# Attention inside an expert pipeline: turned probabilities and value sums by pairs of tiles

## The reference, cut to what matters

```python
x = x + attn(cond(x, ...), ...)          # scores, causal mask, softmax, value sums, W_o
h = einsum('bsd,bdh->bsh', x, W[cat_ids]) + b[cat_ids]
for wg, wu, wdn, cw in experts:          # all 64, weighted by a routing that is zero for most
    y += cw[:, None] * ((silu(h @ wg) * (h @ wu)) @ wdn)
x = x + y + shared(h)
```

## Time and profile before

| | us |
|---|---|
| median of 3 runs | 749.6 (747.75 to 752.17) |
| the profiled execution | 748.22 |
| its span | 746.4 |
| PE busy | 721.3 (97%) |
| DVE, ACT, POOL busy | 549.0, 453.5, 425.1 |
| mean granted clock of TensorE | 0.995 of full |

### The profile page before, as it was taken

The page is one execution under the profiler, slowest core; times in us unless marked ns, Lnnn a source line. Parts: engine busy times, 40 slices in busy tenths (PEclk is TensorE's granted clock), DMA queues, the critical chain, the costliest instruction groups (busy, mean ns, idle before and its releaser), DMA issues.

```text
span 746.4 us, 15904 instructions
## 1 busy us (share of the span) xinstructions
PE 721.3 (97%) x5680; PEld 560.0 (75%) x5680; DVE 549.0 (74%) x1150; ACT 453.5 (61%) x873; POOL 425.1 (57%) x349
## 2 busy tenths in 40 slices
PE   8877999999999999999999999999999999999997
PEld 6765776677777777777787777777777777887885
DVE  5796668886698756976778766987668766886664
ACT  3755865477556675567555774566754675555553
POOL 2528667566456545655555654666446564566665
PEclk9999999999999999999999999999999999999999
DMA  7495443435534453444564344443634345345441
GB/s 264 141 356 135 123 121 99 127 94 156 120 107 118 123 144 109 129 103 127 125 117 134 98 150 113 120 113 120 141 113 135 103 125 128 102 125 141 128 134 46
DMA packets 69055, 97.21 MB, mean 130 GB/s; under 512 B 8016, under 2 KB 26896, under 8 KB 68976
## 3 DMA queue, kind: packets, MB, share of 16 engines
q1 hardware_dynamic: 64512, 91.21, 44.1%
q10 hardware_dynamic: 4464, 4.98, 1.9%
HBM read 90.73 MB, written 4.98 MB: 128 GB/s over the span
## 4 chain that ended last, share of the span: by engine, by line
PE 73%; DVE 11%; ACT 10%; issue 3%; POOL 2%; POOLq 0%; DVEq 0%; ACTq 0%
PE U L967 20%; PE Y L967 20%; PE G L967 19%; PE A L967 12%; DVE act_w L938 3%; POOL hid_lo L631 2%; ACT s_t L395 2%; ACT hid_hi L532 2%; DVE hid L950 2%; ACT L520 1%; ACT L395 1%; DVE k_blk L678 1%; ACT G L520 1%; PE A L1031 1%; DVE spread_p L861 1%
## 5 line engine op out<-in xcount | busy, mean ns | idle before, releaser
L631 POOL TENSOR_TENSOR hid_lo<-hid,hid_hi 128x512 fp32r<-128x512 f32 (+1 forms) x264 | 342.1, 1296 | 275.1 <-ACT hid_hi L532 274.0
L938 DVE TENSOR_TENSOR act_w<-G,cwb 128x512 f32<-128x512 f32 x248 | 170.4, 687 | 100.3 <-ACT G L520 99.3
L520 ACT ACTIVATE G<-G 128x512 f32<-128x512 f32 x248 | 144.4, 582 | 140.6 <-PE G L967 137.7
L532 ACT CAST hid_hi<-hid 128x512 fp32r<-128x512 f32 (+1 forms) x264 | 162.4, 615 | 71.8 <-DVE hid L950 70.5
L950 DVE TENSOR_TENSOR hid<-act_w,U 128x512 f32<-128x512 f32 (+1 forms) x256 | 175.8, 687 | 24.1 <-PE Y L967 1.5
L967 PE MATMUL Y<-hid_hi,wd_hi 128*128 128x512 f32 (+1 forms) x264 | 107.0, 405 | 5.4 <-POOL hid_lo L631 5.1
L967 PE MATMUL G<-c_hi,wg_hi 128*128 128x512 f32 x248 | 111.8, 451 | 0.2 <-DVE act_w L938 0.2
L967 PE MATMUL Y<-hid_hi,wd_lo 128*128 128x512 f32 (+1 forms) x264 | 103.6, 393 | 0.0
L967 PE MATMUL Y<-hid_lo,wd_hi 128*128 128x512 f32 (+1 forms) x264 | 103.4, 392 | 0.0
L967 PE MATMUL U<-c_hi,wu_hi 128*128 128x512 f32 x248 | 99.0, 399 | 1.1 <-DVE hid L950 1.1
L967 PE MATMUL G<-c_lo,wg_hi 128*128 128x512 f32 x248 | 97.5, 393 | 0.0
(11 more groups left out here) (191 smaller groups left out, 900.0 us busy)
## 6 DMA issues: line engine op xcount, KB each, us to landing
cwb<-cw_scratch SPq DMA_DIRECT2D x256, 256.0 KB, 3.7
k_blk<-in_cond_w SPq DMA_DIRECT2D x112, 64.0 KB, 2.4
wg_raw<-in_we_gate SPq DMA_DIRECT2D x8, 256.0 KB, 6.0
wu_raw<-in_we_up SPq DMA_DIRECT2D x8, 256.0 KB, 6.2
wd_raw<-in_we_down SPq DMA_DIRECT2D x8, 256.0 KB, 6.6
xf<-in_x_feat SPq DMA_DIRECT2D x8, 256.0 KB, 4.2
out_feat<-y ACTq DMA_DIRECT2D x8, 256.0 KB, 3.6
h_feat<-pooled_scratch SPq DMA_DIRECT2D x7, 256.0 KB, 2.7
```

Source lines behind the costliest of these rows:

```text
L520: nc.scalar.activation(gate_bank(p)[:, :], gate_bank(p)[:, :], ACT.Silu).then_inc(S["silu_done"], 1)
L532: nc.scalar.copy(hid_hi[0:n, p % NH, :], hid[0:n, p % NH, :]).then_inc(S["hi_ready"], 1)
L631: nc.gpsimd.tensor_sub(hid_lo[0:n, p % NH, :], hid[0:n, p % NH, :], hid_hi[0:n, p % NH, :].bitcast(F32)).then_inc(S["lo_ready"], 1)
L938: nc.vector.tensor_mul(act_w[:, p % NH, :], gate_bank(p)[:, :], cwb[:, p % NCW, :])\
```

## The change

For all blocks but the opening one, the tiles are taken by twos. Step 12 (unit 7) turns tiles 0 and 1, into A1 and A2. Step 14 (unit 9) sums the values of tiles 0 and 1, both into A0 side by side, and turns tiles 2 and 3. Step 16 (unit 11) sums the values of tiles 2 and 3. Units 8 and 10 have no attention work on PE any more. ACT copies two tiles in step 12 and two in step 14. DVE divides two tiles at a time, in steps 14 and 16: one reciprocal over 128x32, one product over 128x256. Since A2 is now written in unit 7, the wait for the hidden tile of unit 6 stands there.

```diff
                 act.wait_ge(S["probT_ps"], blk * TILES + t + 1)
                 if t >= 2:
-                    act.wait_ge(S["av_ps"], blk * TILES + t - 1)
-                nc.scalar.copy(pt_sb[:, t % 2, :], (G[1] if opening(blk) else A1)[:, :]).then_inc(S["probT_ready"], 1)
+                    act.wait_ge(S["av_ps"], t - 1 if opening(blk) else blk * TILES + 2)
+                nc.scalar.copy(pt_sb[:, t % 2, :], (G[1] if opening(blk) else (A1, A2)[t % 2])[:, :]).then_inc(S["probT_ready"], 1)
...
-                elif 12 <= p < 16 and not opening(blk):
-                    turned_probs(p - 12, blk)
+                elif p in (12, 14) and not opening(blk):
+                    for t in (p - 12, p - 11):
+                        turned_probs(t, blk)
...
+                elif p in (14, 16):
+                    pair = slice(p - 14, p - 12)
+                    ps = A0[:, 0:2 * HEADS * VC].rearrange("p (t h m) -> p t h m", t=2, m=VC)
+                    dve.wait_ge(S["av_ps"], blk * TILES + p - 12)
...
+            def turn_probs(pair, blk):
+
+                pe.wait_ge(S["prob_tile"], blk * TILES + pair[1] + 1)
+                pe.wait_ge(S["probT_ready"], blk * TILES + pair[0])
+                for t in pair:
+                    for g in range(NG):
+                        last = nc.tensor.transpose((A1, A2)[t % 2][:, bass.ts(g, P)], s_t[:, t, bass.ts(g, P)], C["ident"])
+                    last.then_inc(S["probT_ps"], 1)
+
+            def value_sums(pair, blk):
+
+                pe.wait_ge(S["probT_ready"], blk * TILES + pair[1] + 1)
+                pe.wait_ge(S["weighted"], blk * NPAIR + LENT + 1)
+                for t in pair:
+                    for g in range(NG):
+                        for r in range(SPT):
+                            at = (t % 2) * HEADS * VC + g * HG * VC
+                            last = mm(A0[32 * r:32 * r + 32, at:at + HG * VC],
+                                      pt_sb[:, t % 2, g * P + 32 * r:g * P + 32 * r + 32], v_blk[:, t, r, g, :])
+                last.then_inc(S["av_ps"], 2)
...
+                elif p == 16:
+                    pe.wait_ge(S["att_ready"], blk * TILES + 2)
+                    value_sums((2, 3), blk)
+                elif p == 14 and not opening(blk):
+                    value_sums((0, 1), blk)
+                    turn_probs((2, 3), blk)
+                elif p == 12 and not opening(blk):
+                    pe.wait_ge(S["biased_tile"], blk * TILES + TILES)
+                    pe.wait_ge(S["hid_ready"], (blk - 1) * UNITS + LENT + 1)
+                    turn_probs((0, 1), blk)
```

More of the change, by code:

```diff
@@ L694, in attention_step @@
                     nc.vector.tensor_reduce(head_max[:, t, :], s, AX, ALU.max).then_inc(S["biased_tile"], 1)
-                elif 13 <= p < 17:
+                elif 13 <= p < 17 and opening(blk):
                     t = p - 13
@@ L703, in attention_step @@
                         .then_inc(S["att_ready"], 1)
+                elif p in (14, 16):
+                    pair = slice(p - 14, p - 12)
+                    ps = A0[:, 0:2 * HEADS * VC].rearrange("p (t h m) -> p t h m", t=2, m=VC)
+                    dve.wait_ge(S["av_ps"], blk * TILES + p - 12)
+                    steps[0] += 2
+                    nc.vector.reciprocal(rden[:, pair, :], ps[:, :, :, HD]).then_inc(S["dve_chain"], 2)
+                    dve.wait_ge(S["dve_chain"], blk * CHAIN + steps[0])
+                    nc.vector.tensor_mul(att[:, pair, :, :], ps[:, :, :, 0:HD],
+                                         rden[:, pair, :].unsqueeze(3).to_broadcast([P, 2, HEADS, HD]))\
+                        .then_inc(S["att_ready"], 2)
                 elif p == 18:
@@ L1021, in attention_step @@
                         last.then_inc(S["score_tile_ps"], 1)
-                if 12 <= p < 16:
+                if 12 <= p < 16 and opening(blk):
                     t = p - 12
@@ L1032, in attention_step @@
                     last.then_inc(S["probT_ps"], 1)
-                if 13 <= p < 17:
+                if 13 <= p < 17 and opening(blk):
                     t = p - 13
```

## The result

The change makes the kernel slower: 773.08 us (median; 771.77 to 774.92) against 748.67 us for the kernel before beside it (four runs), a ratio of 1.033 with a 95% interval of 1.0306 to 1.0353. The profiled execution took 771.77 us, with a span of 769.9.

A forecast was written before the change was run, and what follows sets the result against it. PE, busy for 97% of the span, was taken as the bound. 12.3 us for seven blocks plus 3.2 for two clock falls, on the profiled 748.2, gave 763.7; with 1.4 more for medians, 765.1 us, range 759 to 773.

The forecast's parts named there:

- The new wait: In unit 7, before its first transposes, PE stands still 3.24 us per block until unit 6's hidden tile is done.
- The groups: Attention work on PE, doubled in units 7, 9 and 11, goes from 4.2 to 3.6 us per block.
- What is late next: ACT rounds unit 6's hidden tile later, behind two copies; PE's down product of unit 6 waits 0.1 us, at most 0.4.
- The sum without the clock: Units 7 to 12 take 17.4 us against 15.64: 1.76 more per block, 12.3 for seven.
- The clock: Behind the waits in unit 7 PE's clock may fall to half, 1.6 us each; two of seven taken, 3.2 us.
- the second rival: PE's clock falls after five to seven of the unit 7 waits: 769.9 us for five, 773.1 for seven; chance 0.20.

The follow-up runs named there:

- the wait alone: The kernel before with only the wait for unit 6's hidden tile added in unit 7, its five groups unchanged: 769.15 us, ratio 1.0298.
- the filled wait: The change with 12 narrow matmuls that nobody reads put in front of the wait in unit 7: 760.02 us, ratio 1.0166.

## Why the prediction was right and wrong

- **The new wait** was right: 3.24 us by the prediction, 3.26 in the third stretch (269.93 to 273.19) and 3.25 to 3.40 in the seven, released by the hidden tile of unit 6.
- **The groups** were right: unit 9 takes 1.74 us by the same count (280.84 to 283.04 less two steps of 0.23; taken: 1.8) and unit 11, counted alike, 0.91 (taken: 1.0). That the pairs save 0.6 us per block was forecast, and the wait alone beside the filled wait shows it (17.9 against 17.35).
- **What is late next** was right within its bounds: 0.1 us was taken for the down product of unit 6. The change has no wait there, but its PE came late by the half clock; with the filled wait, at full clock, the step behind that product's first matmul is 0.09 us longer than others (274.89 to 275.21, against 0.23).
- **The sum without the clock**, 12.3 us, is what the filled wait measured: 12.3 by the medians, 11.6 by the stretches.
- **The clock** is the step that failed: "I take two: 3.2" of seven falls. All seven waits fell, and the falls cost 12.7 us (12.1 by the medians). Five stretches are 1.4 to 1.5 us longer than with the filled wait (18.83 against 17.33), near the 1.6 at which the earlier trace rows priced a fall; two are 2.75 longer (20.06 against 17.31), with a slow part of 6.91 us at 0.56 where the first stretch has 4.05 at 0.59, which no row of before showed. 748.67 + 12.3 + 12.7 is 773.7, against 773.08 measured.

So the time lies 8 us above the forecast, just above the range's end. What came about is the second rival, with all seven falls (773.1, chance 0.20). That its number meets 773.08 is in part luck: it starts from 749.6, 0.9 above the 748.67 measured beside the change, and prices the seven falls at 11.2 us for 12.7. The choice of two had no row behind it: the prediction laid the wait between the one fall and the one stretch without a fall in the earlier trace rows, called it nearer to the first, and then took fewer than half. The gap before the one fall had 2.45 us without matmuls out of 2.94, and in the other stretch PE was busy for over half of the time; by these rows more than two falls were the likelier case. That it would be all seven no row could tell, nor do the runs make it a rule.

Of the rule of the Trainium skill ("TensorE: Matmul & The Clock Gate", "Why this matters for your kernels", no long gaps between bursts) the change's trace shows what it says: seven gaps, seven falls. As a rule on the single gap the runs do not bear it out: the same gap in the kernel before fell once in seven in its trace, and shorter ones (2.5 us) six times in seven. As a warning of a price it holds in every run here with 2.1 us of standing or more.

## What to carry to other kernels

When a bank is lent out, the wait for its owner moves with the first write; find the moment at which PE comes to it, and put ahead of it the work that does not need the bank (742.5 us here) rather than the work that does (773). On an engine that sets the end, count a new gap between dense work twice: as the time that it stands and as a possible slow stretch behind it, here 1.3 to 2.75 us for 3.3 us of standing, and let the range reach to all of them. Where such a gap can't be avoided, products that nobody reads may pay: 2.7 us of them per gap took 12 to 13 us from this kernel.

## What was not expected of the hardware

More work on PE made the kernel faster, by 12 to 13 us (12 narrow matmuls in each wait); 3 in each block, far from the wait, at least made it no slower. Waits of 3.2 to 3.4 us were followed by half clock seven times in seven, five in seven and once in seven, in kernels that differ by the order or by 0.7 us of work per block; waits of 2.5 us six times in seven, and 2.1 us of standing twice in seven, each in one execution. In the change's first stretch half clock came only when PE had been back at work for most of a microsecond. A narrow f32 matmul of 128 columns took 0.223 us, as much as one of the wide ones with 512 columns (0.23).
